# A four-layer mixture-of-experts kernel: one set of x rows in memory, earlier b2 rows, masks moved into the first blocks, and expert 0 always first in layers 1 and 2

## The reference

```python
x = x + L0_ffn(L0_cond(x))   # adapter and layernorm; 8 experts, top-p 0.8, relu, 256 -> 1024 -> 256
x = x + L1_ffn(L1_cond(x))   # masked softmax pooling over the sequence; 8 experts, top 1, gelu, 1024
x = x + L2_ffn(L2_cond(x))   # linear by category; 8 experts, top 1, gelu, hidden 512
x = x + L3_ffn(L3_cond(x))   # linear by category; 32 experts, top 6, and a shared one
# layer 1's router:
logits = z @ Wr + br
idx = argmax(logits, -1)     # each token goes to one expert
out[token] = softmax(logits)[idx] * (gelu(z @ W1[idx] + b1[idx]) @ W2[idx] + b2[idx])
```

## Time and profile before

| | |
|---|---|
| median of 3 runs | 1335.82 us (1334.29 to 1337.52) |
| the profiled execution's own time | 1337.58 us |
| its span | 1335.9 us |
| mean granted clock of TensorE | 0.916 of full speed |
| busy share: PE, DVE, ACT, POOL | 85%, 74%, 49%, 37% |

### The profile page before, as it was taken

How to read it: one execution, slowest core, us unless ns; L and a number is a source line. 1 busy time by engine, 2 the same in 40 slices (tenths; PEclk the granted TensorE clock), 3 DMA queues, 4 the chain that set the end, 5 groups by cost and what they waited for, 6 DMA issues and landing times.

```text
span 1335.9 us, 26939 instructions
## 1 busy us (share of the span) xinstructions
PE 1138.6 (85%) x8142; PEld 1057.5 (79%) x8142; DVE 989.0 (74%) x1721; ACT 651.8 (49%) x1361; POOL 500.0 (37%) x341
## 2 busy tenths in 40 slices
PE   5788959999999999999477489978479686899997
PEld 3677848999999999999446389977379665788886
DVE  6656967888888888888576587756468648777775
ACT  3433336667776677766044276622157352122222
POOL 5000026888888788786200234420057400000000
PEclk8899969999999999999778689998589887999999
DMA  7400435777777767775501276523078500000001
GB/s 188 148 23 2 174 127 165 232 236 216 238 242 241 237 217 231 236 244 147 147 6 64 82 265 244 200 81 104 24 230 263 171 30 1 24 25 24 24 24 63
DMA packets 77172, 188.28 MB, mean 141 GB/s; under 512 B 14147, under 2 KB 52291, under 8 KB 64835
## 3 DMA queue, kind: packets, MB, share of 16 engines
q1 hardware_dynamic: 55394, 148.06, 32.5%
q0 software_dynamic: 21728, 39.65, 12.2%
HBM read 157.18 MB, written 30.49 MB: 140 GB/s over the span
## 4 chain that ended last, share of the span: by engine, by line
PE 68%; DVE 15%; issue 8%; DMA 5%; ACT 2%; POOL 1%; DVEq 1%; SPq 0%; POOLq 0%; ACTq 0%
PE ps L678 22%; PE ps L679 21%; PE ps L680 21%; PE ps L802 2%; DVE hidden_lo L1416 2%; DMA scratch<-in_L_w 1%; DVE x_tok L1786 1%; DVE featA_lo L1416 1%; PE ps L690 1%; DMA y_rows<-w_raw,slot_rows 1%; DVE x_tok L1742 1%; DMA b_block<-in_L_ffn_b 1%; DVE w_lo L1416 1%; DVE hidden_f L1775 1%; DMA z_tok<-y_rows 1%
## 5 line engine op out<-in xcount | busy, mean ns | idle before, releaser
L1215 ACT ACTIVATE hidden_f<-ps,b_block 128x256 f32<-128x256 f32 x432 | 221.4, 513 | 177.9 <-PE ps L680 168.5
L582 POOL DMA_INDIRECT x_tok<-z_gate_rows,slot_rows x76 | 210.6, 2771 | 231.3 <-DVE slot_rows L1570 155.8
L1416 DVE TENSOR_TENSOR hidden_lo<-hidden_f,hidden_hi 128x512 fp32r<-128x512 f32 x300 | 195.3, 692 | 68.2 <-ACT hidden_hi L1252 36.6
L1216 ACT ACTIVATE hidden_hi<-ps,b_block 128x256 fp32r<-128x256 f32 x432 | 223.2, 517 | 0.0
L678 PE MATMUL ps<-w_hi,featA_hi 128*128 128x256 f32 (+1 forms) x624 | 178.7, 286 | 7.4 <-DVE w_lo L1416 3.4
L679 PE MATMUL ps<-w_lo,featA_hi 128*128 128x256 f32 (+1 forms) x624 | 177.7, 285 | 0.0
L680 PE MATMUL ps<-w_hi,featA_lo 128*128 128x256 f32 (+1 forms) x624 | 177.7, 285 | 0.0
L678 PE MATMUL ps<-featB_hi,hidden_hi 128*128 128x256 f32 x608 | 173.3, 285 | 0.0
L679 PE MATMUL ps<-featB_lo,hidden_hi 128*128 128x256 f32 x608 | 171.4, 282 | 0.0
L680 PE MATMUL ps<-featB_hi,hidden_lo 128*128 128x256 f32 x608 | 170.3, 280 | 0.0
L608 POOL DMA_INDIRECT x_rows<-w_raw,slot_rows x76 | 124.6, 1639 | 37.2 <-issue 21.9
(11 more groups left out here) (386 smaller groups left out, 3143.8 us busy)
## 6 DMA issues: line engine op xcount, KB each, us to landing
scratch<-in_L_w SPq DMA_DIRECT2D x48, 1024.0 KB
z_tok<-in_L_w SPq DMA_DIRECT2D x29, 1024.0 KB
x_tok<-in_L_w SPq DMA_DIRECT2D x19, 1024.0 KB
b_block<-in_L_ffn_b POOLq DMA_DIRECT2D x60, 128.0 KB, 3.6
z_tok<-in_L_w SPq DMA_DIRECT2D x12, 512.0 KB
scratch<-in_L_w SPq DMA_DIRECT2D x12, 512.0 KB
z_rows<-z_tok SPq DMA_DIRECT2D x8, 512.0 KB, 2.9
z_tok<-y_rows SPq DMA_DIRECT2D x8, 512.0 KB, 5.5
```

Of the source, the lines that this page charges most:

```text
L582: gp.indirect_dma_start(XBL[L][:, k, tt, :], None, ZD if L else ZD0, bass.IndirectOffsetOnAxis(ap=TOK[:, q * BTT + tt:q * BTT + tt + 1], a ...
L1215: act.activation(HF[:, f // 2, part], ps, func, bias=b1)
L1216: act.activation(HTh[:, k, f // 2, part], ps, func, bias=b1).then_inc(s_hhi[L], 1)
L1416: return nc.vector.tensor_tensor(out, full, hi.bitcast(F32), ALU.subtract)
```

## The change

- **One set of x rows.** `XD` is one DRAM tensor. Expert 0's gated output takes X with it when it is formed (a `scalar_tensor_tensor` for a `tensor_scalar`), is stored once, and all scatters accumulate onto it. The store of all of X into `XD[0]` goes. A scatter waits for the scatter of the block before it. At the end of layer 0 SP makes 4 loads for 8, and no add stands between them and the transposes.
- **b2 rows.** POOL asks for the two first b2 rows ahead of the gathers of step 1.
- **Masks.** The router splits, `cond_split(1)` and the first part of the masks (`pool_modes`) stand between `x_lo(0, 0)` and `lows(0, 0)` of layer 0; the rest (`pool_masks`) between the gate columns and the loop. W2 of block 1 is loaded into the upper half of X, so its load moves behind the last x store, and that behind the landing of the first gathers.
- **Expert 0 first.** A table `THR` holds 256 k, but -1 for expert 0 and k = 0: expert 0 has at least one block. For layers 1 and 2 its W1 is loaded into the hidden buffer after the last `lows` of the layer before, and split by ScalarE and VectorE into `W1F`. SP loads block 1's W1 first.
- **Order at the start of layers 1 and 2.** `slot_tokens` stands ahead of the gates' sums; ScalarE loads gelu's table before the block list; the second block's rows are transposed and split in the middle of the first block's `hidden`; `w2_split(0, 0)` follows `lows(0, 0)`.

```diff
+        THR = G[:, 0:8, 16:24]
...
             def block_weights(L):
...
-                    load_w2(0, 1, first[1])
                     x_rows(1)
-                    sp.wait_ge(s_out, 16 * 3)
+                    sp.wait_ge(s_out, 16 * 2)
                     load_w1(0, 0, first[0])
                     x_rows(2)
+                    for k in range(2):
+                        sp.wait_ge(s_xb[0][k], 16 * BTT)
                     x_rows(3)
+                    load_w2(0, 1, first[1])
                 else:
+                    second = expert(0, 1)
                     sp.wait_ge(s_zd, ZD_IN[L])
-                    load_w1(0, 0, first[0])
+                    load_w1(0, 1, second)
                     for k in range(2):
                         sp.wait_ge(s_xb[L][k], 16 * BTT)
-                    load_w1(0, 1, first[1])
-                    for k in range(2):
-                        load_w2(0, k, first[k])
+                    load_w2(0, 0, 0)
+                    load_w2(0, 1, second)
+                    sp.wait_ge(s_gate, L + 1)
...
+                if L < 2:
+                    sp.wait_ge(s_hlo[L], steps * NF + H0[L])
+                    first_w1(L + 1)
...
-                    for rows, dst in ((YD, Z),) if L else ((XD[0], X), (XD[1], Z)):
+                    rows, dst = (YD, Z) if L else (XD, X)
...
             def scatter_add(i, k):
                 q = i * 2 + k
+                if q:
+                    gp.wait_ge(s_yst[0][1 - k], 16 * BTT * (i + k))
...
             def first_rows(L):
...
                 gp.wait_ge(s_list, L + 1)
+                for k in range(2):
+                    bias(L, 0, k)
+                gp.sem_inc(s_yb[L], 2)
                 steps = gp.value_load(BLK[L][0:1, 63:64], min_val=1, max_val=STEPS[L])
                 with gp.If(steps > 1):
                     for k in range(2):
                         gather(L, 1, k)
-                for k in range(2):
-                    bias(L, 0, k)
-                gp.sem_inc(s_yb[L], 2)
...
             def order(L):
...
-                link(nc.vector.tensor_scalar(even, IO[:, 0:8], float(BT), None, ALU.mult))
-                link(nc.vector.tensor_tensor(cmp, count.broadcast_to([P, 8, 8]),
-                                             even.unsqueeze(1).broadcast_to([P, 8, 8]), ALU.is_gt))
+                link(nc.vector.tensor_tensor(cmp, count.broadcast_to([P, 8, 8]), THR, ALU.is_gt))
...
+            link(nc.vector.tensor_scalar(THR, IO[:, 0:8].unsqueeze(1).broadcast_to([P, 8, 8]), float(BT), None, ALU.mult))
+            link(nc.vector.memset(THR[:, 0:1, 0:1], -1.0))
...
             def y0_gated(u, g):
...
-                    nc.vector.tensor_scalar(Z[:, n, :], Z[:, n, :], G[:, n, 0:1], None, ALU.mult).then_inc(s_yfree, 1)
+                    nc.vector.scalar_tensor_tensor(Z[:, n, :], Z[:, n, :], G[:, n, 0:1], X[:, n, :],
+                                                   ALU.mult, ALU.add).then_inc(s_yfree, 1)
...
+            def first_w1(L):
+                n = KD * LAYERS[L][1]
+                dve.wait_ge(s_w1hi[L], 1)
+                lo(W1F[1][:, 0:n], HFf[:, 0:n], W1F[0][:, 0:n]).then_inc(s_w1sp[L], 1)
...
-            add_back(0, "x1", TAh, TAl)
+            transposes("x1", TAh, TAl)
```

More of the change, by code:

```diff
@@ L106, in build @@
         ZD0 = nc.dram_tensor("z0_gate_rows", [ROWS, ZW0], F32).ap()
-        XD = [nc.dram_tensor(f"x_rows{k}", [ROWS, D], F32).ap() for k in range(2)]
+        XD = nc.dram_tensor("x_rows", [ROWS, D], F32).ap()
         ZD = nc.dram_tensor("z_rows", [ROWS, D], F32).ap()
@@ L411, in first_expert @@
                 half_weights(1)
-                for c in range(1, NC):
-                    sp.wait_ge(s_x[c], 16)
-                sp.dma_start(XD[0][0:B * SEQ].rearrange("(t p) d -> p t d", p=P), X[:]).then_inc(s_out, 16)
                 z_rows(2)
@@ L807, in hidden @@
                     q = i * 2 + k
+                    w1h, w1l = W1F if first and L else (x[:, k, :] for x in WB1[L])
                     pe.wait_ge(s_xlo[L], q + 1)
@@ L810, in hidden @@
                     for f in range(NF):
+                        if first and f == NF // 2:
+                            trans(0, 1)
                         if not first or f >= 4:
@@ L1207, in hidden @@
                     for f in range(NF):
+                        if first and f == NF // 2:
+                            xt(0, 1)
                         act.wait_ge(s_hps[L], NF * q + (H0[L] + f + 1))
@@ L1332, in _ @@
             blocks(0)
+            first_w1(1)
             transposes("x1", TAh)
@@ L1506, in order @@
                 cmp = SC[:, 2, ET:ET + 64].rearrange("p (e k) -> p e k", k=8)
-                own, upto, even = (SC[:, 2, 256 + 8 * k:264 + 8 * k] for k in range(3))
+                own, upto = (SC[:, 2, 256 + 8 * k:264 + 8 * k] for k in range(2))
                 dve.wait_ge(s_rank, L + 1)
@@ L1662, in lows @@
                     for f in range(NF // 2):
+                        if isinstance(q, int) and q == 0 and f == NF // 4:
+                            x_lo(1, 1)
                         dve.wait_ge(s_hhi[L], NF * q + (H0[L] + 2 * f + 2))
@@ L1703, in blocks @@
                     x_lo(0, 0)
+                    for n in range(1, 4):
+                        router_split(n)
+                    cond_split(1, [(P, slice(0, KD * A0))])
+                    pool_modes()
                 else:
                     x_lo(0, 0)
-                    first_splits(L)
+                    w1_lo(1, 1)
                 lows(0, 0)
-                x_lo(1, 1)
+                if L:
+                    w2_split(0, 0)
                 if L == 0:
@@ L1711, in blocks @@
                     gate_column(0, 1)
+                    own = pool_masks()
                 with dve.Fori(0, STEPS[L]) as i:
@@ L2110, in _ @@
             y0_gated(7, 1)
-            blocks(0)
-            for L in range(1, 4):
-                router_split(L)
-            own = pool_masks()
-            cond_split(1, [(P, slice(0, KD * A0))])
+            own = blocks(0)
+            first_w1(1)
             link(nc.vector.tensor_copy(SC[0:A0, 7, 0:P], V1[:].broadcast_to([A0, P])))
             dve.sem_inc(s_clo, 1)
-            add_back(0, "x1", TAh, TAl)
+            transposes("x1", TAh, TAl)
             nc.vector.tensor_copy(XRh[:, :, D:D + 2], ONE[:, 0:2].unsqueeze(1).broadcast_to([P, NT, 2]))
```

96 lines of the change are left out of this document (55 added, 41 removed).

## The result

The changed kernel takes 1349.07 us (median of 4 runs, 1347.94 to 1350.87) beside 1335.24 for the kernel before: 1.0102 times as long, 95% interval 1.0085 to 1.012. It is slower by some 13.8 us, where the forecast was 3.0 and the range ended at 1347. Run again on a second chip it took 1.0077 times as long (1.0049 to 1.0104), 1350.74 beside 1340.8.

The account below looks back on a forecast made before the run. The prediction took TensorE to bound the block loops, with gains only where it stands still. Terms of 23.8 - 10.4 - 7.4 - 5.7 + 2.7 = +3.0 us on the median of 1335.82 gave 1338.8; range 1331 to 1347.

Parts of the forecast that it names:

- Term 1: Layer 1's loop: expert 0's empty block makes 6 steps for 5, one extra step, +23.8 us.
- Term 2: Seam from layer 0 to 1: fewer loads and no adds let the transposes and next matmuls start earlier, -10.4 us.
- Term 3: Start of layer 1's blocks: TensorE's 5.75 us standstill goes and step 1's hidden starts earlier, -7.4 us.
- what is late next is VectorE: Start of layer 1's blocks: VectorE's chain of splits and lows ends at 785.8, and step 1's hidden starts there.
- rival B: Starts of layers 1 and 2 gain half, as loads end later: +6.5 us in all, 1345.3; chance 0.2.
- Term 4: Start of layer 2's blocks: the 4.93 us wait goes and VectorE's chain lets step 1 start earlier, -5.7 us.
- Term 5: Start of layer 0's blocks: masks on VectorE's chain delay step 1's hidden, against an earlier first hidden, +2.7 us.
- the 5 us of waiting for VectorE: Layer 0's start: TensorE stands still about 5 us for VectorE ahead of step 1's hidden.
- POOL's wait for the scatter before costs nothing: Block loops: the scatter's new wait costs nothing, since POOL already waited for the same semaphore in `buffer_left`.
- stay slow: Layer 0's start: gathers keep their lengths beside VectorE's subtractions; by the other reading the sum would be 0.5 lower.

Follow-up runs that it names:

- masks at the seam: 24 mask instructions moved behind layer 0's loop, against the version with expert 0 first in layer 2 alone and layer 1's W1 copy earlier: 1322.66 us, 0.9852 of the kernel before.

## Why the prediction was wrong

Its sign was right, its size was not: 3.0 forecast, 13.8 measured.

- **Term 1 was right**: 24 scatters, 23.83 us a step, +23.9 in the ledger, and the version without the forced block gets it back.
- **Term 2 was right in its own stretch**, -10.3 for -10.4. Two small errors cancel: the last scatter is 0.8 later, and the stretch behind the transposes gains 3.1 for the 2.6 taken. **The step that failed is the one left unsaid**: that all behind the seam moves forward unchanged. The pooling took 3.6 us more, at a granted clock of 0.63 in both profiles, for 0.79 and 0.69 before. That the clock is the cause is shown (VectorE's and ScalarE's busy times are the same, TensorE's is not). That the change brings it is not: of six profiles of kernels that are identical up to there but for the b2 rows, four took 39.8 to 40.0 us and two 36.7 (granted clock 0.74), and the kernel before took 34.9 and 37.7. What decides it is open.
- **Term 3 was mis-sized**, -4.7 for -7.4: -3.5 in the first pair and -6.0 in the second. The step "what is late next is VectorE" failed: neither profile has the wait for `x_lo` ahead of step 1 that it asked for. Next was W1 of step 1, which lands 8.9 to 11.8 us after SP asks for it with three loads beside it. ScalarE, in order, holds up the evictions of hidden (0, 1) for it. The price of that wait was in rival B. The size varies: in four more profiles with this order hidden (1, 0) starts 54.4 to 55.0 us behind the router, as in the second profile of the change (54.6), for 57.6 in the first and 61.0 and 60.6 before the change. So the gain was mostly about 6 of the 7.4, and the first profile, with the latest load, is the low end. (Its terms also add up to 785.3, not 785.8.)
- **Term 4 was mis-sized**, -1.7 for -5.7. The first block went as forecast: from the first transposes to output (0, 0) took 11.6 us for 16.9 (means of two profiles). But from there to output (1, 0) took 18.4 for 13.6. The load of step 1's W1 makes ScalarE wait 2.4 and 3.0 us and VectorE, behind it, 1.4 and 2.0. So TensorE's wait moved from ahead of hidden (0, 1) (4.93) to ahead of hidden (1, 0) (3.07 and 3.68), and the slow hidden behind it moved along: 5.1 us or more at 1.2 GHz, where the one behind the old wait took 4.6 at a granted clock of 0.63. The step that failed: the chain of VectorE was priced from its own instructions alone.
- **Term 5 was about right**, +2.0 for +2.7. The masks' 6.8 us are on VectorE's chain. But the 5 us of waiting for VectorE were not there as forecast: 2.45 are VectorE's, and 3.3 more ScalarE's, for a load and its copy. That the two together come near the sum is partly luck. The sentence that POOL's wait for the scatter before costs nothing held in the loop (413.3 us from output (1, 0) to the end in the first pair, 413.6 and 413.3 in the second).
- **Rival B** (the starts gain half) had the mechanism and, in these profiles, the size: 6.4 measured for 13.1 forecast. It gives 1345.3; the pooling's 3.6 on top gives 1348.9, near the result. This close a match is partly luck, as term 3 mostly reached more than half, and the pooling differs by 3.3 us between profiles of the same program text. The range fell short because it held no case of B together with a loss in a stretch that the change doesn't touch.

The prediction let the gathers "stay slow" by a rule of the Trainium skill's "SBUF — State Buffer", section "SBUF: two separate sides". What locks GpSimd out of writing descriptors there is a VectorE operation that uses both port pairs, and the same section of the Trainium skill infers that a `tensor_tensor` doesn't. The trace agrees that VectorE holds up a gather, and not that a `tensor_tensor` doesn't: beside `tensor_tensor` alone gathers took 1.9 to 2.4 us (rows in the last section). The same section of the Trainium skill also has an instruction with two inputs in SBUF contend with a GpSimd instruction that reads SBUF; a gather's row numbers lie there, but no run here tells whether that is the reason. So the prediction was right by its rows, and used the rule for more than it states of writing descriptors.

## What to carry to other kernels

A block list that always begins with a fixed expert can cost a whole step of the loop where that expert is empty: count the blocks with the data, round as the loop does, and price the step before any of the gains. When a wait goes at a start, follow every engine's queue and every load to the next wait, not the busiest engine alone; here each gain of a start ended at a load that an in-order engine had ahead of its evictions or of another engine's work. Work moved to fill a stall must stand in the stall itself: VectorE's 5.41 us lay behind the low parts that TensorE waits for, the 24 masks were put ahead of them, and cost 2 us or more there. Behind layer 0's loop they cost 0.4, once the W1 split in front of them was gone.

## What the runs showed of the hardware

- The same instructions of the pooling took 36.7 or 40.0 us, at a mean granted clock of TensorE of 0.74 or 0.63, and one kernel's seven runs lay between 1322.0 and 1331.7. By these two numbers I wouldn't read a difference of less than 0.3% between two medians here (an estimate).
- The length of a wait alone doesn't tell TensorE's clock behind it. Ahead of hidden (1, 0) of layer 2, waits of 1.6 us (three profiles) left it at 2.4 GHz, and so did 2.90 and 3.50 us (24 matmuls in 3.1 us, granted clock 1.00). Waits of 2.91, 3.07, 3.68 and 3.85 us left it at 0.50 to 0.53 for the whole hidden (5.1 us and more), 2.64, 2.79 and 3.91 at 0.65.
- Gathers issued while VectorE ran a 128x2048 subtraction with two inputs ended 0.8 us behind it: after the change at 185.09 and 187.29, behind subtractions that end at 184.26 and 186.46. Where a cast of 128x2048 followed the subtraction, as at 205.15 before the change, the gather ended 0.1 us behind the cast (206.49 and 206.37). The gathers of step 1, issued beside the short mask instructions, took 0.95 to 1.04, with weight loads in flight both times (before the change the same four took 0.95, 3.04, 2.72 and 0.95). With the masks gone again (masks at the seam) the three issued while VectorE stood still took 0.95 to 1.00, and the fourth, beside a subtraction and a cast of 128x2048, 3.01. Timelines of POOL and VectorE after the change:

```profile
182.69 2.40 POOL L597 DMA_INDIRECT x_tok<-z_gate_rows,slot_rows  x1 [0.30 <-issue]
185.40 1.89 POOL L597 DMA_INDIRECT x_tok<-z_gate_rows,slot_rows  x1 [0.30 <-issue]
...
201.30 0.98 POOL L597 DMA_INDIRECT x_tok<-z_gate_rows,slot_rows  x1 [0.31 <-issue]
```

```profile
181.97 2.29 DVE L1450 TENSOR_TENSOR featA_lo<-z_tok,featA_hi 128x2048 fp32r<-128x2048 f32 x1
184.18 2.28 DVE L1450 TENSOR_TENSOR featB_lo<-scratch,featB_hi 128x2048 fp32r<-128x2048 f32 x1
```
